# Who issues the pieces of keys: ScalarE's queue instead of SyncE's, and the first row maxima half a tile sooner

## The reference

```python
x = _layernorm(x + _L0_attn_ref(x, ...))   # causal attention, 16 heads of 128
x = _layernorm(x + _L0_ffn_ref(x, ...))    # 8 experts, top 2, and a shared block of 704
x = _layernorm(x + _L1_attn_ref(x, ...))   # 16 heads of 16, 4 groups of keys and values
x = _layernorm(x + _L1_ffn_ref(x, ...))    # 16 experts, top 6, and a shared block of 352
```

```python
sh = jax.nn.silu(x @ sw_gate) * (x @ sw_up)           # 256 -> 704
shared_out = sh @ sw_down                             # 704 -> 256
...
q, k, v = jnp.split(x @ Wqkv + bqkv, [D, D + KV], axis=-1)   # second layer
scores = jnp.einsum('bqhd,bkhd->bhqk', q, k) / HD
prob = jax.nn.softmax(scores, axis=-1)
```

## Time and profile before

| | before |
|---|---|
| median of 3 executions | 2080.97 us (2077.53 to 2086.6) |
| profiled execution, its own time | 2084.41 us |
| its span, first to last instruction | 2082.7 us |
| mean granted clock of TensorE | 0.989 |
| busy share PE, DVE, ACT, POOL | 96%, 68%, 58%, 30% |
| call "f2" of `shared_half`, first to last matmul | 1138.4 to 1222.3 us |

### The profile page before, as it was taken

The page is one execution under the profiler, slowest core; times in us unless marked ns, Lnnn a source line. Parts: engine busy times, 40 slices in busy tenths (PEclk is TensorE's granted clock), DMA queues, the critical chain, the costliest instruction groups (busy, mean ns, idle before and its releaser), DMA issues. The chain is left out here.

```text
span 2082.7 us, 34448 instructions
## 1 busy us (share of the span) xinstructions
PE 2008.7 (96%) x12163; PEld 1549.1 (74%) x12163; DVE 1418.6 (68%) x2853; ACT 1210.7 (58%) x2488; POOL 627.4 (30%) x739
## 2 busy tenths in 40 slices
PE   8999999999999999998889989999999999999997
PEld 6888888888888888886788663333334788788886
DVE  5666667666776677675657569999992556655555
ACT  5656666666665566665435437888886434444343
POOL 3444444444443346554333510000000212222221
PEclk9999999999999999999999979999999999999999
DMA  2310000000000001004344301101000111111111
GB/s 77 100 51 21 21 21 21 21 9 21 21 22 14 21 21 38 30 19 101 93 151 121 82 21 32 24 17 25 17 9 17 36 38 46 46 45 39 53 46 58
DMA packets 74221, 86.90 MB, mean 42 GB/s; under 512 B 12443, under 2 KB 54086, under 8 KB 74054
## 3 DMA queue, kind: packets, MB, share of 16 engines
q1 hardware_dynamic: 70982, 76.32, 13.0%
q0 software_dynamic: 3072, 8.39, 1.3%
HBM read 58.32 MB, written 18.35 MB: 37 GB/s over the span
## 5 line engine op out<-in xcount | busy, mean ns | idle before, releaser
L1155 POOL TENSOR_TENSOR a_pr<-a_pr,a_rinv 128x512 f32<-128x512 f32 (+3 forms) x384 | 312.7, 829 | 452.3 <-DVE a_rinv L1412 451.7
L91 PE MATMUL psum<-xh,g_hi_gu 128*128 128x512 f32 x744 | 305.4, 410 | 11.0 <-PEq L59 3.8
L2860 ACT ACTIVATE a_pt<-psum 128x512 f32<-128x512 f32 x512 | 276.3, 597 | 59.1 <-PE psum L2760 35.5
L2879 DVE TENSOR_REDUCE x_m_negm<-psum 128x1 f32<-128x1024 f32 x240 | 290.7, 1223 | 13.6 <-PE psum L2745 11.3
L93 PE MATMUL psum<-xh,g_lo_gu 128*128 128x512 f32 x744 | 292.6, 393 | 0.0
L92 PE MATMUL psum<-xl,g_hi_gu 128*128 128x512 f32 x744 | 291.8, 392 | 0.0
L1503 POOL TENSOR_TENSOR g_lo_gu<-g_raw_gu,g_hi_gu 128x512 fp32r<-128x512 f32 x62 | 80.2, 1294 | 625.7 <-ACT g_hi_gu L1499 625.6
L1317 ACT ACTIVATE a_pr<-psum,a_negm 128x128 f32<-128x128 f32 (+7 forms) x256 | 190.3, 743 | 100.2 <-DVE a_negm L1402 96.3
L1324 ACT ACTIVATE a_pth<-psum 128x512 fp32r<-128x512 f32 (+3 forms) x384 | 174.9, 490 | 109.9 <-PE psum L1221 105.4
L1419 DVE TENSOR_TENSOR a_ptl<-psum,a_pth 128x512 fp32r<-128x512 f32 (+3 forms) x384 | 201.1, 551 | 1.1 <-ACT a_pth L1324 0.9
L1402 DVE CUSTOM_DVE_ANT_0 psum<-psum,a_mask 128x128 f32<-128x128 f32 (+7 forms) x256 | 191.7, 749 | 1.3 <-PE psum L93 0.2
(11 more groups left out here) (403 smaller groups left out, 4679.4 us busy)
## 6 DMA issues: line engine op xcount, KB each, us to landing
g_raw_gu<-in_gu SPq DMA_DIRECT2D x60, 256.0 KB, 2.8
g_raw_gu<-in_qkv SPq DMA_DIRECT2D x32, 256.0 KB, 2.8
f_raw_dn<-in_down SPq DMA_DIRECT2D x60, 128.0 KB, 2.0
xs<-a_mask SPq DMA_DIRECT2D x2, 2944.0 KB, 10.8
ys<-e_yb SPq DMA_DIRECT2D x46, 128.0 KB
a_wvr<-in_qkv SPq DMA_DIRECT2D x32, 128.0 KB, 2.4
a_wor<-in_o SPq DMA_DIRECT2D x32, 128.0 KB, 2.0
x_queries_qq<-x_qhi SPq DMA_DIRECT2D x128, 32.0 KB, 1.9
```

What stands on the lines that cost most here:

```text
L91: pe.matmul(out, a_hi, b_hi, start=first, stop=False)
L1155: pool.tensor_tensor(x, x, rinv[:, j:j + 1].to_broadcast([P, count * P]), ALU.mult).then_inc(p_done, 1)
L2860: act.activation(pt[:, s % SLOTS, g, :], st_ps[:, n % 3, :], ACT.Exp, scale=1.0 / HD1).then_inc(exp_done, 1)
L2879: dve.tensor_reduce(negm[:, u % 2, g * NQ + q:g * NQ + q + 1], mx_ps[:, bank, :, :], AX.XY, ALU.max, negate=True).then_inc(mx_taken, 1)
```

## The change

There are three edits. `QKVHalf.sync` takes which rows r to issue. SyncE's call in step K = 2 is gone; ScalarE issues the six pieces of r = 0 in tile 1 after `round_gu(2)`, and the six of r = 1 in the same tile after `round_dn(1)` and the side tasks of (1, 0, 1). The maxima are planned without the offset: n = 0 to 3 in tile 2, and four in each of tiles 3, 4 and 5, none in the drain. The later call of `sync` in `grouped_attention`, for the other half, is unchanged.

```diff
-    def sync(self, sp, ring=None):
-        sp.wait_ge(self.cleared, 1)
+    def sync(self, dma, ring=None, rows=range(2)):
+        dma.wait_ge(self.cleared, 1)
         if ring is not None:
-            sp.wait_ge(ring.emptied, ring.count((self.name, ("pj", 2, 1))))
-        for r in range(2):
+            dma.wait_ge(ring.emptied, ring.count((self.name, ("pj", 2, 1))))
+        for r in rows:
             for x, src in enumerate((self.khi, self.klo, self.khi)):
                 for g in range(2):
                     p0, d0 = r * HALFP + x * HD1, (r * 2 + g) * HD1
-                    sp.dma_start(self.ks[p0:p0 + HD1, g, :].bitcast(F32), src[d0:d0 + HD1, :].bitcast(F32)).then_inc(self.k_in, 16)
+                    dma.dma_start(self.ks[p0:p0 + HD1, g, :].bitcast(F32), src[d0:d0 + HD1, :].bitcast(F32)).then_inc(self.k_in, 16)
...
                 if experts:
                     experts.load(sp, 2 * K - 2)
                     experts.load(sp, 2 * K - 1)
-                for o in begins:
-                    if isinstance(o, QKVHalf) and K == 2:
-                        o.sync(sp, ring)
...
                 if 2 <= K + 1 <= LAST:
                     round_gu(K + 1)
+                for o in begins:
+                    if isinstance(o, QKVHalf) and K == 1:
+                        o.sync(act, ring, rows=(0,))
                 if K <= LAST:
                     keep_hi(K, 0)
...
                 for side, t in plan.get((K, 0, 1), ()):
                     side.scalar(act, t, ring)
+                for o in begins:
+                    if isinstance(o, QKVHalf) and K == 1:
+                        o.sync(act, ring, rows=(1,))
                 for side, t in plan.get((K, 1, 0), ()):
...
                     for n in range(m0.COUNT):
-                        plan[2 + (n + 2) // 4, (n + 2) // 2 % 2, n % 2] = [(m0, (0, n)), (m0, (1, n))]
+                        plan[2 + n // 4, n // 2 % 2, n % 2] = [(m0, (0, n)), (m0, (1, n))]
```

## The result

| | before | after |
|---|---|---|
| median of 20 executions each, on one chip in turns | 2086.22 us (2076.73 to 2097.75) | 2095.66 us (2083.97 to 2113.26) |
| profiled execution, its own time (span) | 2084.41 (2082.7) us | 2087.93 (2086.2) us |
| mean granted clock of the profiled execution | 0.989 | 0.985 |

The ratio is 1.0042, with a 95% interval of 1.0023 to 1.0061: slower by 0.4%, inside the 0.5% that the prediction called no change, but a real loss of some 9 us where 0.5 us of gain was forecast, and 2095.66 lies above the range's 2087. The pair of profiled executions shows only 3.5 us of it in the span. So there are two things to explain: the 3.5 us between these two traces, and the rest, which they don't hold.

A forecast was written before the change was run, and what follows sets the result against it. TensorE's order of work and four waits for VectorE (7.7 us) were taken to bound the block's end. Drain -3.7, pairs +1.5 and key wait +1.65 gave -0.55 us, so 2080.4 us, range 2074 to 2087.

The forecast's parts named there:

- The price of an issue on ScalarE, 0.63: Each piece of keys on ScalarE's queue was taken to cost 0.63 us, as on SyncE; bounds 0.1 and 1.26.
- The rivals of a free and of a dearer issue: Pieces on ScalarE's queue: at 0.1 each, 2079.4 us, chance 0.18; at higher prices, up to 2088 to 2090, chance 0.17.
- the dearer one: Pieces at 1.26 each on ScalarE: silu 3.7 late, keys holding TensorE another 4.9, +6.9 us, about +9 with lower clock; chance 0.17.
- The silu: Tile 1's second half, behind ScalarE's first six pieces: done at 1159.8, before TensorE wants its bank at 1159.94, so hidden.
- Gain in the drain, 3.7: End of the block: two pairs of maxima matmuls (2.3) and a wait (1.4) leave, so it ends 3.7 us sooner.
- Two pairs in tile 2, 1.5: First half of tile 2 on TensorE: two added pairs of maxima matmuls cost 0.75 us each at full clock, 1.5 together.
- lands 2.35 to 2.4 later: Last piece of keys, issued at 1162.05, lands at 1164.4, so tile 2's first maximum, ready at 1162.75, waits 1.65 us.
- SyncE ... can go a little sooner ... nothing is gained: SyncE loses 8.2 us of issue; its weights for tiles 3 and 4 go sooner, but no listed wait is for a transfer.
- the gain gets little: Clock rival: low clock at the block's end lifts, 2076, chance 0.15 for 4 us or more; tile 2's fall may cost 1.7.
- The other three waits ... I leave them as they are: TensorE's waits for VectorE in tiles 3, 4 and 5 only shift with everything else and stay at about 2 us.
- a sign that it is wrong: Prediction wrong if the silu holds TensorE, VectorE's later waits change by the shift, or the low stretch at the end goes.
- The rule of the Trainium skill: Pieces moved to ScalarE's queue: another issuing engine saves only sequencer time, usually small; the prediction noted twelve issues took 8.2 us.

The follow-up runs named there:

- e2: Changed kernel with the maxima back in their old places, ScalarE still issuing the twelve pieces of keys; ratio to the kernel before 0.9992 (0.9975 to 1.0009).
- e1: Kernel before with only the maxima half a tile sooner, SyncE still issuing the pieces; key wait 0.1 us, ratio to before 1.0023 (1.0004 to 1.0042).
- e4: Changed kernel without GpSimd's four gathers of tile 1; key wait 2.1 us, ratio to the kernel before 1.0014 (0.9990 to 1.0038).
- e6: Changed kernel with SyncE's weights of tiles 3 and 4 held until the keys are in; key wait 2.0 us, ratio to before 1.0019 (1.0000 to 1.0038).
- e13: Changed kernel without tile 1's gathers and with SyncE's weights held until the keys are in; key wait 1.1 us, ratio to before 1.0021 (0.9998 to 1.0043).
- e7: The changed kernel measured again, unaltered, beside the kernel before; key wait 3.4 us, 2094.28 against 2081.25 us, ratio 1.0051 (1.0030 to 1.0071).
- e12: Changed kernel with maxima in old places, TensorE made to wait for the keys before tile 2's first down product; ratio to before 1.0040 (1.0022 to 1.0058).
- e3: Changed kernel with six pieces (r = 0) on ScalarE and six on SyncE at the old place; no key wait, ratio to before 1.0006 (0.9984 to 1.0028).
- e15: Repeat of the changed kernel with six pieces on each of ScalarE's and SyncE's queues; no key wait, ratio to before 1.0001 (0.9978 to 1.0025).
- e10: Changed kernel with eight unread matmuls in the attention's first four steps; ratio to before 1.0031 (1.0011 to 1.0050), without one execution of 4930.86 us.

## Why the prediction was wrong, point by point

- *The price of an issue on ScalarE, 0.63.* Right: 0.63. The rivals of a free and of a dearer issue fall; what the dearer one said would follow, keys that come late and a lower clock behind the wait, came all the same. The silu was hidden, too: done at 1159.23 against 1159.8 worked out.
- *Gain in the drain, 3.7.* Right for this pair of profiles, 3.71, and too much for the kernel: both have the drain at the low clock. At the full clock the same two distances are 5.69 in e2 (old order) and 3.51 in e1 (new), a gain of 2.2:

```profile
1208.07 0.73 PE L1575 MATMUL psum<-x_ks,x_queries_qq 48*128 48x512 f32 x2
...
1213.76 0.40 PE L2205 MATMUL psum<-f_hh,f_lo_dn 128*128 128x512 f32 x1
```

```profile
1206.89 0.73 PE L1575 MATMUL psum<-x_ks,x_queries_qq 48*128 48x512 f32 x2
...
1210.40 0.40 PE L2208 MATMUL psum<-f_hh,f_lo_dn 128*128 128x512 f32 x1
```

  Less the 1.5 for the pairs in tile 2 this leaves 0.7 us, so even without a key wait there was next to nothing to gain. I took the price from an execution whose drain ran at the low clock.
- *Two pairs in tile 2, 1.5.* Right at the full clock: the tile's last two pairs take 0.66 each (1178.32 to 1178.98), with a gap of 0.1 ahead. The first two ran at the low clock, which is in the 4.5 below.
- *"lands 2.35 to 2.4 later".* **The term that was mis-sized.** The last pieces took 4.8 us, so the wait was 3.58 and not 1.65. I took the landing from a place where nothing else moved. e4, e6 and e13 show what was in the way: the gathers that stay beside the pieces, and the weights of the queue that was freed.
- *"SyncE ... can go a little sooner ... nothing is gained".* Wrong as a dismissal: nothing was gained, and the keys came some 1.4 us later for it. The 8.2 us taken from SyncE put the weights' transfers into the last keys' time (e6).
- *The clock: "the gain gets little", a fall behind the new wait of "some 1.7 us".* **The step that failed.** It was up to 4.5 in the profiled execution and no term of the sum held it, and over the executions the clock holds 8 to 10 of e7's 11.4 us. With the measured wait the sum without the clock is -3.7 + 1.5 + 3.58 = +1.4, or about +2.9 with the drain's gain at the full clock (2.2), against e7's rest of 1.4 to 3.4: so the order of the engines' work explains the smaller part and the clock the larger. That a wait of 3.5 us alone brings a loss that can't be told from the change's is shown by e12, and that the loss goes with the wait by e3 and e15. Why the changed kernel has 21 to 26 us of low clock in the block, and not only the 3 to 10 right behind the wait, stays open.
- *"The other three waits ... I leave them as they are".* Two stayed at 2.17 and 1.96; tile 3's went from 2.19 to 0.48, which the prediction itself had named as a sign that it is wrong. The rows of VectorE say why. In the kernel before:

```profile
1172.68 2.69 DVE L2318 TENSOR_TENSOR f_hl<-f_hid,f_hh 128x512 fp32r<-128x512 f32 x1 [1.54 <-issue]
```

and on GpSimd beside it:

```profile
1172.29 1.29 POOL L672 TENSOR_TENSOR g_z<-g_z 128x512 f32<-128x512 f32 x1
1173.53 1.29 POOL L1503 TENSOR_TENSOR g_lo_gu<-g_raw_gu,g_hi_gu 128x512 fp32r<-128x512 f32 x1
```

In the changed kernel, VectorE and then GpSimd:

```profile
1181.92 0.98 DVE L2321 TENSOR_TENSOR f_hl<-f_hid,f_hh 128x512 fp32r<-128x512 f32 x1 [1.55 <-issue]
```

```profile
1181.04 1.31 POOL L672 TENSOR_TENSOR g_z<-g_z 128x512 f32<-128x512 f32 x1
1182.49 1.57 POOL L1503 TENSOR_TENSOR g_lo_gu<-g_raw_gu,g_hi_gu 128x512 fp32r<-128x512 f32 x1
```

The same remainder takes 0.68 us elsewhere. Before, it ran beside two operations of GpSimd and took 2.69; after, it met the last 0.4 us of the first and took 0.98, and that 1.71 less is the 1.71 by which the wait shrank. That they hinder each other is read from rows, no run tried it. The Trainium skill says in "SBUF — State Buffer", section "Terms", that VectorE and GpSimd share a pair of ports which one of them holds for a whole instruction; the trace agrees in so far as the remainder of 2.69 ends 0.55 after GpSimd's second operation (1175.37 against 1174.82), and the one of 0.98 also 0.55 after the operation that it met (1182.90 against 1182.35). It was luck of the shift, and is in none of my terms; e10, the same block, has that wait at 2.17 again. Without the luck this execution would have been some 5.2 us longer, not 3.5.

- *The rule of the Trainium skill* ("DMA: Bandwidth & Descriptors", section "Issuing engines are not separate DMA queues"), that another issuing engine saves only the sequencer's time, agrees with these runs: SyncE's 8.2 us of issue became some 7.6 on ScalarE, and e2's ratio is 0.9992.

## What to carry to other kernels

The landing time of a transfer isn't a constant: take it with what else is in flight at that moment, and count what the queue that you free will send in its place. Where an order on TensorE is nearly full, a new wait of some 3 us is to be priced above itself, since the clock can fall behind it: in e12 a wait of 3.5 us cost 6.8 us in the mean, with 4.6 to 12 us as the interval of its ratio. A loss by the clock shows in many executions with the clock of each, not in one pair of profiles; the pair here held 3.5 us of 9, because the profiled execution of before had much low clock of its own in this block. So look at a second profile of the kernel before, and take no price from a stretch at the low clock unless the others have it too.

## What the runs showed of the hardware

The clock can stay at the low level while TensorE has no idle time: 27.30 us busy of 27.30 at 0.50 in e7, behind 12.9 us at the full clock with 12.50 busy. And 64 KB pieces that take 2.4 us to land with neither gathers nor weights beside them took 4.8 on ScalarE's queue beside both (3.5 and 3.4 with one of them away), and 2.8 on SyncE's queue with the weights behind.
